# Gather of the up factors: tiles go round all eight PSUM banks, four copies of a T move from VectorE to ScalarE, and one sum goes ahead of the first copies

## The chip, the cores and the metric

The kernel runs on 1 core of one Trainium2 chip. The metric is the device time of one execution in microseconds. Engines are named as in the profile: PE is TensorE's matmul, PEld its weight load, DVE is VectorE, ACT is ScalarE, POOL is GpSimd, SP the engine that issues the DMAs. A name with a q behind it (PEldq) is the sequencer of that engine: it computes registers, waits for semaphores, branches, and hands the matmuls on.

## What is computed

A block of a perceiver on 32 sequences of 64 rows of 512 numbers: cross attention to 1601 context rows, causal self attention, and a mixture of experts whose weights are Kronecker factors. In the reference's words, cut to what matters here:

```python
x = x + xattn(layernorm(x), ctx_1024, ...)
x = x + attn(layernorm(x), ...)
x = x + ffn(layernorm(x), ...)

def kmoe(x_flat, W_router, A, B, scale, bias, ...):      # 2048 rows of 1024 numbers
    logits = x_flat @ W_router.T                          # 64 experts
    vals, idx = jax.lax.top_k(logits, top_k)              # top_k = 2
    probs = jax.nn.softmax(vals, axis=-1)
    xs = x_flat.reshape(-1, d_in1, d_in2)
    Ag = A[idx]
    Bg = B[idx]
    Y = jnp.einsum('nkoi,nij,nkpj->nkop', Ag, xs, Bg)
    out = jnp.einsum('nkop,nk->nop', Y, probs).reshape(-1, d_out1 * d_out2)
    return out * scale + bias
```

ffn is kmoe up (32x32 to 64x64), an exact gelu, and kmoe down (64x64 to 32x32). The change is in how Ag and Bg of the up layer are fetched.

## The kernel before

All engines run programs of their own that meet at semaphores; nothing is scheduled by a planner, the order on each engine is the order of the code. Cross attention comes first, then self attention over eight quads of rows, then the mixture. The last quad's output projection leaves its two halves in PSUM banks 2 and 3; VectorE adds them to the rows (`with_attended`, line 838, counted by the semaphore `se_r2`). A sum with the output bias (line 842), the layer norm and the stores of that last quad are done by VectorE inside the first part of the mixture.

The up layer runs for T = 0 to 3, 256 tokens with two experts each. Every T begins with a gather. A one-hot of the tokens' choices is multiplied by the experts' tables, so that PSUM holds the chosen factors: v = 0 is the factor A, v = 1 the factor B, q = 0 to 7 is an eighth of the table. So a T has 16 tiles, in the order (q, v). A tile is 32 matmuls (line 2222) into two banks, one for each half hf. Then hf 0 is copied to SBUF by ScalarE (line 2104) and hf 1 by VectorE (line 1947). The tile (q, v) uses banks 4v and 4v + 1, in each q again. Thus four banks are in use, and a tile waits until the copies of the tile two before it are done: `gather_up` waits for `s_geu` of both engines (`mo_geu0`, `mo_geu1`) at the tile's count less two. It also waits for `s_ts`: GpSimd has laid the tile's part of the table (line 1836) into one of two buffers.

PE's gather is a loop in hardware: one turn is two q, that is four tiles, and four turns are a T. All its counts are computed in registers. `apart` puts a step of its own before the tile's first matmul that carries the last waits (line 50 in the profile).

Behind the loop PE waits for the down layer's one-hots of the T before (`mo_ohedn0`, `mo_ohedn1`: they were transposed into banks 6 and 7) and, but for the last T, for `se_r2`. It then transposes the next T's rows (`rows`, line 1490) into ROW_BANKS, banks 2, 3, 6 and 7, which the gather doesn't use. It waits for the last copies of the gather. For T > 0 it computes the down router's logits of the T before in banks 0 and 1 (`logits_dn(0)`, line 2200; VectorE's `parts` reads them), and then the next T's up router (line 1506) and the 16 steps of the two contractions (lines 2239 and 2257), which use all banks.

VectorE's program in a T: for T > 0 one half of the rows is transposed (2.2 us) before the first copy, and a quarter of the other half (0.7 us) after the copies of q = 1, 2, 3 and 4. For T = 0, `with_attended` for bank 3 stands behind the two copies of q = 0, and the two sums of line 842 behind q = 2 and q = 4.

Of the kernel before, what the change touches and what calls it, by code (L numbers as in the profile page):

```python
# [27 lines left out]
P = 128  # L28
# [87 lines left out]
class Signals:  # L116


    CREDIT = 8
# [1147 lines left out]
def mixture_parts(sem, arena, over, area, low, top_area, early, ps, ident, h_at, tables):  # L1267
# [53 lines left out]
    ROW_BANKS = (2, 3, 6, 7)  # L1321
# [32 lines left out]
    def gathered_up(v, q, hf):  # L1354

        dst = fac[v].rearrange("p (m o) -> p m o", o=F1)[:, :, 32 * hf + 4 * q:32 * hf + 4 * q + 4]
        return dst, ps[:, 4 * v + hf, :].rearrange("p (o m) -> p m o", o=4)
# [224 lines left out]
    f.ROW_BANKS = ROW_BANKS  # L1582
# [70 lines left out]
def mixture(nc, block, arena, early, ps, a, first, rest, out):  # L1653
# [41 lines left out]
    ROW_BANKS = first.ROW_BANKS  # L1695
# [241 lines left out]
    def _(vec):  # L1937
# [4 lines left out]
        def gather_out(T, q, v):  # L1942
            if T and q == 0:
                vec.wait_ge((s_sta, s_stb)[v], STEPS * T + AHEAD)
            vec.wait_ge(s_gu, 16 * T + 2 * q + v + 1)
            dst, src = gathered_up(v, q, 1)
            vec.tensor_copy(dst, src).then_inc(s_geu[1], 1)
# [56 lines left out]
        for T in range(T_N):  # L2004
            if T:
                transposed(vec, T, 0)
            for q in range(8):
                for v in range(2):
                    gather_out(T, q, v)
                if T and 1 <= q <= 4:  # L2010
                    transposed(vec, T, 1, q - 1, 4)
                if T == 0:
                    if q == 0:
                        rest.with_attended(vec, 1)
                    if q == 2:
                        rest.with_output_bias(vec, 0)
                    if q == 4:
                        rest.with_output_bias(vec, 1)
# [4 lines left out]
            if T:  # L2023
                parts(T, 0)
# [73 lines left out]
    def _(act):  # L2098
        def gather_out(T, q, v):
            if T and q == 0:  # L2100
                act.wait_ge((s_sta, s_stb)[v], STEPS * T + AHEAD)
            act.wait_ge(s_gu, 16 * T + 2 * q + v + 1)
            dst, src = gathered_up(v, q, 0)
# [90 lines left out]
    def _(pe):  # L2194
# [16 lines left out]
        def gather_up(v, g):  # L2211

            pe.wait_ge(s_ts, g * 2 + v + 1)
            for e in range(2):
                pe.wait_ge(s_geu[e], g * 2 + v - 1 + CREDIT)
            apart(pe, SPARE)
            for o in range(4):
                for c in range(C):
                    for hf in range(2):
                        r = slice(hf * E, (hf + 1) * E)  # L2220
                        x = ohx_up[r, 0, :, c * R:(c + 1) * R] if v == 0 else ohx_b[r, c % 2, c // 2]
                        last = pe.matmul(ps[c * R:(c + 1) * R, 4 * v + hf, o * P:(o + 1) * P],  # L2222
# [131 lines left out]
        with pe.Fori(0, T_N) as T:  # L2354
# [4 lines left out]
            with pe.Fori(T * 4, T * 4 + 4) as j:  # L2359
                for r in range(2):  # L2360
                    gather_up(0, j * 2 + r)
                    gather_up(1, j * 2 + r)
            for e in range(2):
                pe.wait_ge(s_ohe["dn"][e], T - 1 + CREDIT)
            with pe.If(T < T_N - 1):
                pe.wait_ge(rest.r2, rest.r2_all)
                for t in range(2):
                    rows(pe, T + 1, t, ROW_BANKS[2 * t:2 * t + 2])
            for e in range(2):
                pe.wait_ge(s_geu[e], T * 16 + 16 + CREDIT)  # L2370
            with pe.If(T > 0):
# [3 lines left out]
                logits_dn(0)  # L2375
# [70 lines left out]
```

## Time and profile before

| | us |
|---|---|
| median of 3 runs | 1257.72 |
| lowest and highest | 1257.55, 1258.91 |
| the profiled execution's own time | 1257.94 |
| its span | 1255.9 |
| gather of T = 0, 1, 2, 3, first matmul from the span's start | 837.43, 895.95, 954.25, 1013.50 |

The profile is one execution. PE is busy for 1194.3 us of the span, DVE 799.6, ACT 435.9, POOL 274.4. Cross attention takes the first two fifths, self attention ends near 837 us, the up layer near 1067 us, and the down layer the rest. A timeline merges instructions of one line that follow each other closely; xN counts records, and one matmul of the gather leaves two records on PE, so 64 records are a tile. In brackets stands the idle time of the engine before the row, and what ended it. The sequencer's steps are not counted as busy; the view of a line shows them with their own duration (minimum, median, maximum), but not the time between one and the next.

### The profile page before, as it was taken

To read this page: it belongs to the slowest core of one execution; us is meant where nothing else is said; L and a number is where in the kernel's file an instruction comes from. 1 tells how busy PE (TensorE), PEld (TensorE's weight loads), DVE (VectorE), ACT (ScalarE), POOL (GpSimd) and SP (SyncE) were. 2 spreads that over 40 slices of the span, in tenths; PEclk is the share of its full clock that TensorE was granted. 3 is DMA by queue.
4 is the path that set the end of the run, shared out by engine and by line. 5 is a ranking of instruction groups with operands and counts; after the bars stand their busy time and mean duration, and the time that the engine had idled before them with its cause. 6 is when DMAs were issued, how large, how long until landed. Compare 5 with 4: busy or idle time off the path is not lost.

```text
span 1255.9 us, 63911 instructions
## 1 busy us (share of the span) xinstructions
PE 1194.3 (95%) x28911; PEld 797.9 (64%) x28911; DVE 799.6 (64%) x1612; ACT 435.9 (35%) x894; POOL 274.4 (22%) x477
## 2 busy tenths in 40 slices
PE   9999999999999999999999999997898988899995
PEld 6865443444444334666676667766787877789995
DVE  5566787678767773355555555575848576467775
ACT  2322311131113212312221222235656556466664
POOL 1000000000000001112221222114443525245655
PEclk9999999999999999999999999999999999999998
DMA  7887999999999992510111011410413122143423
GB/s 286 277 273 229 313 321 308 303 305 329 301 322 299 321 334 94 120 68 0 67 67 67 7 59 50 126 41 14 166 60 134 67 95 106 38 132 113 122 58 77
DMA packets 64977, 203.09 MB, mean 162 GB/s; under 512 B 12112, under 2 KB 28496, under 8 KB 51440
## 3 DMA queue, kind: packets, MB, share of 16 engines
q1 hardware_dynamic: 64880, 201.77, 49.2%
q8 instruction: 64, 1.05, 0.3%
q14 instruction: 33, 0.27, 0.1%
HBM read 168.18 MB, written 33.55 MB: 161 GB/s over the span
## 4 chain that ended last, share of the span: by engine, by line
PE 84%; DVE 5%; issue 3%; SPq 2%; POOL 2%; DMA 2%; ACT 1%; POOLq 0%; DVEq 0%; ACTq 0%
PE ps L738 14%; PE ps L581 12%; PE ps L1111 9%; PE ps L2222 5%; PE ps L2305 5%; PE ps L2271 5%; PE ps L251 5%; PE ps L1225 4%; PE ps L1132 4%; PE ps L494 3%; PE ps L2200 2%; PE ps L2318 2%; PE ps L2257 2%; DVE arena L1956 2%; DVE arena L593 2%
## 5 line engine op out<-in xcount | busy, mean ns | idle before, releaser
L593 DVE STREAM_TRANSPOSE arena<-arena 128x448 f32<-128x448 f32 (+1 forms) x512 | 258.7, 574 | 54.9 <-DMA arena<-ctx 36.1
L581 PE MATMUL ps<-arena 32*64 32x400 f32 (+1 forms) x4096 | 188.7, 501 | 2.7 <-DVE arena L593 1.9
L738 PE MATMUL ps<-arena 128*64 128x512 f32 x832 | 189.1, 598 | 0.0
L581 PEld LDWEIGHTS ps<-arena 32*64 32x64 f32 x4096 | 81.8, 131 | 102.6 <-DVE arena L593 50.8
L616 ACT ACTIVATE arena<-ps,arena 128x384 f32<-128x384 f32 x64 | 36.3, 581 | 291.3 <-DVE arena L607 291.3
L738 PEld LDWEIGHTS ps<-arena 128*64 128x64 f32 x832 | 55.6, 136 | 121.3 <-issue 121.3
L1111 PE MATMUL ps<-arena 128*128 128x256 f32 x512 | 114.2, 381 | 0.8 <-ACT arena L1046 0.8
L1111 PEld LDWEIGHTS ps<-arena 128*128 128x128 f32 x512 | 96.4, 190 | 17.2 <-issue 3.3
L911 POOL TENSOR_TENSOR arena<-arena 128x1024 f32<-128x1024 f32 x8 | 18.9, 2367 | 390.5 <-PE ps L738 390.5
L2120 ACT COPY arena<-ps 128x512 f32<-128x512 f32 x128 | 75.0, 586 | 50.3 <-PE ps L2271 26.5
L1956 DVE SCALAR_TENSOR_TENSOR arena<-ps,arena 128x512 f32<-128x512 f32 x64 | 69.8, 1120 | 33.7 <-PE ps L2257 33.2
L2222 PE MATMUL ps<-arena 64*32 64x128 f32 x4096 | 68.7, 273 | 7.9 <-issue 4.4
L2271 PE MATMUL ps<-arena 64*64 64x32 f32 x4096 | 71.0, 219 | 3.2 <-issue 3.2
L2271 PEld LDWEIGHTS ps<-arena 64*64 64x64 f32 x4096 | 69.7, 136 | 3.8 <-issue 3.4
L2222 PEld LDWEIGHTS ps<-arena 64*32 64x32 f32 x4096 | 58.1, 105 | 18.9 <-issue 14.7
L1966 DVE COPY arena<-ps 128x512 f32<-128x512 f32 x64 | 44.3, 692 | 37.9 <-PE ps L2305 35.7
L599 DVE TENSOR_REDUCE arena<-ps 128x1 f32<-128x401 f32 (+1 forms) x64 | 32.3, 567 | 54.7 <-PE ps L581 54.7
L979 DVE SCALAR_TENSOR_TENSOR arena<-ps,arena 128x512 f32<-128x512 f32 x32 | 20.6, 686 | 70.1 <-PE ps L1122 70.1
L929 POOL TENSOR_TENSOR arena<-arena 128x512 f32<-128x512 f32 x32 | 33.3, 1042 | 138.6 <-DVE arena L996 138.6
L2305 PE MATMUL ps<-arena 64*64 64x128 f32 x1792 | 62.7, 277 | 0.0
L251 PE MATMUL ps<-arena 128*128 128x512 f32 x128 | 60.2, 605 | 0.0
L1132 PE MATMUL ps<-arena 128*64 128x256 f32 x512 | 59.0, 380 | 0.0
(161 smaller groups left out, 1882.6 us busy)
## 6 DMA issues: line engine op xcount, KB each, us to landing
arena<-ctx SPq DMA_DIRECT2D x64, 1024.0 KB
arena<-ctx SPq DMA_DIRECT2D x32, 768.0 KB
arena<-q_n SPq DMA_DIRECT2D x64, 256.0 KB, 11.3
h_n<-arena SPq DMA_DIRECT2D x12, 1024.0 KB, 4.4
arena<-h_n SPq DMA_DIRECT2D x12, 1024.0 KB, 5.1
arena<-x SPq DMA_DIRECT2D x16, 512.0 KB, 4.4
arena<-ctx SPq DMA_DIRECT2D x32, 256.0 KB
x_n<-arena SPq DMA_DIRECT2D x16, 512.0 KB, 3.5
```

Source lines behind the costliest of these rows:

```text
L251: x = pe.matmul(ps[:, par, :], early.ats[:, c, par::2], early.xwv[:, c, :], start=c == 0, stop=c == DC - 1)
L581: last = pe.matmul(ps[b * SEQ:(b + 1) * SEQ, tb, 0:WIDTH[tb]], qs[p % 2][r, db, b * SEQ:(b + 1) * SEQ], z[PLACE[at]][r, b, 0:WIDTH[tb]], s ...
L593: vec.transpose(z[PLACE[at]][:, :, g * 224:g * 224 + nt * 32].rearrange("p b (j t) -> p b j t", t=32), slots[slot_of(k)][:, :, 0:nt, db * ...
L738: last = pe.matmul(ps[b * SEQ:(b + 1) * SEQ, OB, :], probt[:, j, b * SEQ:(b + 1) * SEQ], slot[:, b, jj, :], start=j == 0, stop=j == TILES - 1)
L1111: last = pe.matmul(ps[:, bank, m % 2 * QROWS:(m % 2 + 1) * QROWS], w[n][:, c, m * P:(m + 1) * P], lnt[:, c, :], start=c == 0, stop=c == DC ...
L1132: last = pe.matmul(ps[e * SEQ:(e + 1) * SEQ, 2 + pair, s2 * 256:(s2 + 1) * 256], lnt[:, c, at:at + SEQ], w["swv"][:, c, :].rearrange("p (m ...
L1225: last = pe.matmul(ps[:, (OUT if more else LAST_OUT) + par, :], aot[:, c, par::2], w["swo"][:, c, :], start=c == 0, stop=c == DC - 1)
L1956: vec.scalar_tensor_tensor(h[:, q, :, at].rearrange("p j g -> p g j"), ps[:, b:b + 2, :].rearrange("p b (g x) -> p (b g) x", x=2 * F1)[:, ...
L2120: act.copy(mid[u].rearrange("p (b x) -> p b x", b=2), ps[:, 2 * u:2 * u + 2, 0:256]).then_inc(s_me, 1)
L2222: last = pe.matmul(ps[c * R:(c + 1) * R, 4 * v + hf, o * P:(o + 1) * P], tab_st[v][r, o, :], x, start=True, stop=True)
L2271: last = pe.matmul(ps[k * F1:(k + 1) * F1, 2 * u + t, g * D1:(g + 1) * D1], st_h[u][rows_t, g * F1:(g + 1) * F1], two(st_a[u])[rows_t, k, ...
L2305: last = pe.matmul(ps[q * E:(q + 1) * E, 6 + hf, o * P:(o + 1) * P], slots_dn[slot][r, o, :], oh_st[r, 2 * q:2 * q + 2, :].rearrange("p k ...
```

## The change

- `ROW_BANKS` becomes (0, 1, 4, 5), and a tile (q, v) uses banks 4v + 2(q mod 2) and the one behind it: four tiles in flight, and a tile waits for the copies of the tile four before it.
- `PAST_DVE = (1, 2, 3, 4)`: for these q the hf 1 copy of v = 1 is made by ScalarE, ahead of its own hf 0 copy. VectorE's count goes up by 2 at its v = 0 copy, so that the counts stay.
- For T = 0, `with_attended` for bank 3 stands ahead of VectorE's first copy.
- On PE the waits for `se_r2` and for the down one-hots stand inside the loop, between its first and second q, since the second q now uses banks 2, 3, 6 and 7. Before each half of `rows` stands a wait for the copies of q = 6.
- `logits_dn` of the loop and `parts` use banks 2 and 3.

```diff
-    ROW_BANKS = (2, 3, 6, 7)
+    ROW_BANKS = (0, 1, 4, 5)
+    PAST_DVE = (1, 2, 3, 4)
@@ gathered_up
-        return dst, ps[:, 4 * v + hf, :].rearrange("p (o m) -> p m o", o=4)
+        return dst, ps[:, 4 * v + 2 * (q % 2) + hf, :].rearrange("p (o m) -> p m o", o=4)
@@ VectorE
             dst, src = gathered_up(v, q, 1)
-            vec.tensor_copy(dst, src).then_inc(s_geu[1], 1)
+            vec.tensor_copy(dst, src).then_inc(s_geu[1], 2 if q in PAST_DVE else 1)
@@
+            if T == 0:
+                rest.with_attended(vec, 1)
             for q in range(8):
-                for v in range(2):
+                for v in range(1 if q in PAST_DVE else 2):
                     gather_out(T, q, v)
                 if T and 1 <= q <= 4:
                     transposed(vec, T, 1, q - 1, 4)
                 if T == 0:
-                    if q == 0:
-                        rest.with_attended(vec, 1)
@@
-                parts(T, 0)
+                parts(T, 2)
@@ ScalarE
             act.wait_ge(s_gu, 16 * T + 2 * q + v + 1)
+            if v and q in PAST_DVE:
+                dst, src = gathered_up(v, q, 1)
+                act.copy(dst, src)
             dst, src = gathered_up(v, q, 0)
             act.copy(dst, src).then_inc(s_geu[0], 1)
@@ PE
-        def gather_up(v, g):
+        def gather_up(v, g, r2):
             pe.wait_ge(s_ts, g * 2 + v + 1)
             for e in range(2):
-                pe.wait_ge(s_geu[e], g * 2 + v - 1 + CREDIT)
+                pe.wait_ge(s_geu[e], g * 2 + v - 3 + CREDIT)
@@
-                        last = pe.matmul(ps[c * R:(c + 1) * R, 4 * v + hf, o * P:(o + 1) * P],
+                        last = pe.matmul(ps[c * R:(c + 1) * R, 4 * v + 2 * r2 + hf, o * P:(o + 1) * P],
@@
             with pe.Fori(T * 4, T * 4 + 4) as j:
-                for r in range(2):
-                    gather_up(0, j * 2 + r)
-                    gather_up(1, j * 2 + r)
-            for e in range(2):
-                pe.wait_ge(s_ohe["dn"][e], T - 1 + CREDIT)
+                gather_up(0, j * 2, 0)
+                gather_up(1, j * 2, 0)
+                pe.wait_ge(rest.r2, rest.r2_all)
+                for e in range(2):
+                    pe.wait_ge(s_ohe["dn"][e], T - 1 + CREDIT)
+                gather_up(0, j * 2 + 1, 1)
+                gather_up(1, j * 2 + 1, 1)
             with pe.If(T < T_N - 1):
-                pe.wait_ge(rest.r2, rest.r2_all)
                 for t in range(2):
+                    for e in range(2):
+                        pe.wait_ge(s_geu[e], T * 16 + 13 + t + CREDIT)
                     rows(pe, T + 1, t, ROW_BANKS[2 * t:2 * t + 2])
@@
-                logits_dn(0)
+                logits_dn(2)
```

PE's program inside the gather's loop, from the second tile of a turn to the third, in the kernel before. An ISA row here is a fused computation of registers. Where a row waits for two semaphores, a step that only waits stands before it and is not listed.

```order
L2213 REGISTER_ALU
L2215 REGISTER_ALU [waits mo_ts]
L2222 MATMUL ps<-arena 32x128 [waits mo_geu0,mo_geu1]
L2222 MATMUL ps<-arena 32x128 x31
L2213 ISA
L2215 REGISTER_ALU [waits mo_ts]
L2222 MATMUL ps<-arena 32x128 [waits mo_geu0,mo_geu1]
L2222 MATMUL ps<-arena 32x128 x31
```

The same place in the changed kernel.

```order
L2217 REGISTER_ALU
L2219 REGISTER_ALU [waits mo_ts]
L2226 MATMUL ps<-arena 32x128 [waits mo_geu0,mo_geu1]
L2226 MATMUL ps<-arena 32x128 x31
L2368 REGISTER_ALU [waits se_r2]
L2217 ISA [waits mo_ohedn1,mo_ohedn0]
L2219 REGISTER_ALU [waits mo_ts]
L2226 MATMUL ps<-arena 32x128 [waits mo_geu0,mo_geu1]
L2226 MATMUL ps<-arena 32x128 x31
```

Two steps of the sequencer have come between these two tiles: the REGISTER_ALU of line 2368 and the unlisted one that waits for `mo_ohedn1`. The other waits ride on steps that were there. From the loop's end to the first matmul of `rows` there are as many steps as before.

VectorE's program at the start of the gather of T = 0, in the kernel before (838 is `with_attended`, 842 the output bias, 1947 a copy out of a tile).

```order
L838 TENSOR_TENSOR arena<-ps,arena 128x512 [waits se_o]
L1936 UNCONDITIONAL_BRANCH
L1947 COPY arena<-ps 128x128x4 [waits mo_gu] x2
L838 TENSOR_TENSOR arena<-ps,arena 128x512 [waits se_o]
L1947 COPY arena<-ps 128x128x4 [waits mo_gu] x4
L842 TENSOR_TENSOR arena<-arena 128x512 [waits se_r2]
L1947 COPY arena<-ps 128x128x4 [waits mo_gu] x4
```

The same place in the changed kernel (the copy is line 1948 there).

```order
L838 TENSOR_TENSOR arena<-ps,arena 128x512 [waits se_o]
L1937 UNCONDITIONAL_BRANCH
L838 TENSOR_TENSOR arena<-ps,arena 128x512 [waits se_o]
L1948 COPY arena<-ps 128x128x4 [waits mo_gu] x4
L842 TENSOR_TENSOR arena<-arena 128x512 [waits se_r2]
L1948 COPY arena<-ps 128x128x4 [waits mo_gu] x2
L842 TENSOR_TENSOR arena<-arena 128x512 [waits se_r2]
```

The second sum now stands ahead of the copies, and fewer copies stand between the sums.

## Rows read from the trace of the kernel before

**Rows 1.** The page: busy time, and the chain that ended last.

```profile
PE 1194.3 (95%) x28911; PEld 797.9 (64%) x28911; DVE 799.6 (64%) x1612; ACT 435.9 (35%) x894; POOL 274.4 (22%) x477
...
PE 84%; DVE 5%; issue 3%; SPq 2%; POOL 2%; DMA 2%; ACT 1%; POOLq 0%; DVEq 0%; ACTq 0%
```

**Rows 2.** Busy time by stretch, one stretch for each T's gather.

```profile
core 0: us, PE busy (x) PEld busy (x) DVE busy (x) ACT busy (x) POOL busy (x), PEclk, DMA share, GB/s
...
895.90:913.90 18.00, 17.08 (x1024) 14.52 (x1024) 13.71 (x20) 9.16 (x15) 4.32 (x15) 1.00 0.46 175
...
1013.50:1032.20 18.70, 17.15 (x1024) 14.50 (x1024) 14.46 (x21) 9.62 (x16) 4.28 (x15) 1.00 0.14 57
```

**Rows 3.** Timeline of PE, T = 1, T = 2 and T = 3.

```profile
start us, us, engine line op out<-in xcount [idle before <-releaser]
...
895.95 4.27 PE L2222 MATMUL ps<-arena 64*32 64x128 f32 x256 [1.82 <-DVE arena L1475]
900.50 4.27 PE L2222 MATMUL ps<-arena 64*32 64x128 f32 x256 [0.28 <-issue]
...
954.25 2.18 PE L2222 MATMUL ps<-arena 64*32 64x128 f32 x128 [0.23 <-issue]
957.11 2.21 PE L2222 MATMUL ps<-arena 64*32 64x128 f32 x128 [0.67 <-DVE arena L1947]
959.61 4.28 PE L2222 MATMUL ps<-arena 64*32 64x128 f32 x256 [0.29 <-issue]
...
1013.50 2.21 PE L2222 MATMUL ps<-arena 64*32 64x128 f32 x128 [0.27 <-issue]
1016.31 2.18 PE L2222 MATMUL ps<-arena 64*32 64x128 f32 x128 [0.59 <-DVE arena L1947]
```

**Rows 4.** Timeline of DVE at the start of T = 2.

```profile
954.24 2.22 DVE L1466 STREAM_TRANSPOSE arena<-arena 128x1024 f32<-128x1024 f32 x1
956.36 1.24 DVE L1947 COPY arena<-ps 128x512 f32<-128x512 f32 x2
```

**Rows 5.** Timeline of ACT in T = 1, tiles 5 to 8.

```profile
902.73 0.58 ACT L2104 COPY arena<-ps 128x512 f32<-128x512 f32 x1 [0.40 <-PE ps L2222]
903.79 0.64 ACT L2104 COPY arena<-ps 128x512 f32<-128x512 f32 x1 [0.47 <-PE ps L2222]
904.82 0.58 ACT L2104 COPY arena<-ps 128x512 f32<-128x512 f32 x1 [0.39 <-PE ps L2222]
906.25 0.64 ACT L2104 COPY arena<-ps 128x512 f32<-128x512 f32 x1 [0.84 <-PE ps L2222]
```

**Rows 6.** Line 2213: PE's sequencer (PEldq) between two tiles.

```profile
L2213 PEldq ALU_OP  x32: 32/32/32, 838.2 to 1030.8; - x32
L2213 PEldq FUSED_REGOPS  x16: 51/51/51, 839.2 to 1029.7; - x16
```

**Rows 7.** Line 2359, one turn of the loop, 899 to 900.5 us.

```profile
L2359 PEldq FUSED_REGOPS  x2: 37/50/64, 899.8 to 900.2; - x2
L2359 PEldq COMPARE_BRANCH  x1: 213/213/213, 899.9 to 899.9; - x1
```

**Rows 8.** Line 2364: the two steps that compute and wait.

```profile
L2364 PEldq ALU_OP  x4: 36/36/36, 856.1 to 1032.1; - x4
L2364 PEldq EVENT_SEMAPHORE  x4: 51/51/51, 856.2 to 1032.2; - x4
```

**Rows 9.** Chain in order of time, T = 1: start, us, what.

```profile
894.42 0.68 DVE arena L1475
895.10 0.85 issue
```

**Rows 10.** Timeline of PE, T = 0: first tiles, then the logits.

```profile
837.43 2.76 PE L2222 MATMUL ps<-arena 64*32 64x128 f32 x160
840.93 1.58 PE L2222 MATMUL ps<-arena 64*32 64x128 f32 x96 [0.74 <-issue]
...
864.02 2.83 PE L1506 MATMUL ps<-arena 128*64 128x128 f32 x24 [2.43 <-issue]
```

More of the change, by code:

```diff
@@ L1581, in mixture_parts @@
     f.ohx_b = ohx_b
-    f.ROW_BANKS = ROW_BANKS
+    f.ROW_BANKS, f.PAST_DVE = ROW_BANKS, PAST_DVE
     f.s_wr = s_wr
@@ L1694, in mixture @@
     ohx_b = first.ohx_b
-    ROW_BANKS = first.ROW_BANKS
+    ROW_BANKS, PAST_DVE = first.ROW_BANKS, first.PAST_DVE
     s_wr = first.s_wr
```

## The prediction

> **What bounds the kernel now.** I read the page first. PE is busy for 95% of the span and carries 84% of the chain that ended last; VectorE carries 5% of it and ScalarE 1% [rows 1]. Work taken from VectorE is worth something only where PE waits for VectorE, and anything that lengthens PE's own program counts in full. Next I read the busy time by stretch: in the gather of T = 1, 18.0 us long, VectorE is busy 13.7 and ScalarE 9.2, and T = 3 is much the same [rows 2]. Neither engine is full. The granted clock is 1.00, the higher of its two levels (2.4 GHz), and nothing here opens a long gap in which it could fall.
>
> Then the timeline of PE, for the waits that end late. In T = 1 a turn of four tiles is busy 4.27 us, the next begins 4.55 us after it, and no turn waits for another engine; the 1.82 us ahead of the first tile is a wait for the one-hots, which the change leaves alone [rows 3]. In T = 2 the third tile waits 0.67 us for VectorE, in T = 3 0.59 us [rows 3]. The timeline of VectorE says why: its 2.22 us transpose runs until 956.46, so the copy of tile 0 begins at 956.36, when tile 1 is nearly done, and with two tiles in flight tile 2 starts only at 957.11 [rows 3, 4]. These two waits are what the wider use of PSUM can remove.
>
> What sets the pace between? ScalarE starts its copy when a tile is complete, so its starts are PE's clock: tile to tile takes 1.03 us from v = 0 to v = 1, 1.06 into the next q, and 1.43 over the loop's turn [rows 5]. The 0.40 between 1.43 and 1.03 can be taken apart. At the short boundary the sequencer runs three steps: 32 and 32 ns of register arithmetic, both of the first kind in [rows 6], and one that waits, 51 ns [rows 8]: 115 ns. At the turn it runs five: two fused ones of 37 and 64 ns, a branch of 213 [rows 7], 36 and 51 as in [rows 8]: 401 ns. That is 286 more and two steps more; if each step also takes 60 ns that no row shows, 286 + 120 = 406 ns, which is the 0.40. The 60 ns has a second witness: between the end of the one-hot copy and the first tile of T = 1 lie 0.85 us [rows 9], in which the sequencer runs seven steps (51, 37, 51, 72, 70, 36, 51 ns by their lines, 368 in all, the kinds of [rows 6 to 8]), and 0.85 - 0.37 over eight spaces is 0.06. So the pace of the gather is set by PE's sequencer: each step put between two tiles is paid in full, because no stock of matmuls bridges it.
>
> **The change part by part.**
>
> *Four tiles in flight.* The two waits go. The second pair of tiles starts 957.11 - 954.25 = 2.86 us after the first in T = 2, and 1016.31 - 1013.50 = 2.81 in T = 3 [rows 3]; at the normal pace it would be 1.03 + 1.06 = 2.09. Gain 0.77 + 0.72 = 1.49 us. What is late next? Tile 4 would have to wait for the copy of tile 0, which ends near 957.0, and begins at 959.61 even now [rows 3, 4]. GpSimd's table takes effect only within its two buffers, as before. So nothing takes the place of these waits.
>
> *Steps inside the loop.* This is the largest term. Between the second and the third tile of each turn the sequencer gets two steps more: one register computation (36 ns) and one that only waits (51 ns) [rows 8], with 60 ns behind each: 0.207 us. There are 4 turns in each of 4 T: 16 x 0.207 = 3.31 us. What they wait for is long there: the down one-hots are of the T before, and `se_r2` is done before the third tile of T = 0 (below). Behind the waiting steps stand only matmuls of the same PE, so the price is theirs alone. In the first turn of T = 0 PE stands idle 0.74 us, two and a half tiles in, for nothing another engine does [rows 10]; I take that as a supply of instructions that is late, and a sequencer that is 0.2 us slower there runs into it 0.2 us less. That takes off between 0 and 0.21; I take 0.1. Bounds for one boundary: below, 0, if the steps hide behind queued matmuls; above, 0.40, what the two further steps of the turn cost now [rows 5]. I take 0.207, since it reproduces both the 0.40 and the 0.85.
>
> *Behind the loop.* The same waits leave this place and others come, step for step, ahead of the first half of `rows`. Before its second half two steps are new, but the first 8 transposes cover them. The copies of q = 6 they ask for are made before the last two tiles end. 0 us, and at most 3 x 0.2 if the cover were gone. T = 3 has no `rows`: two steps fewer, ahead of a wait for the last copies that hides them. 0.
>
> *Four copies to ScalarE.* It makes a hf 1 and a hf 0 copy after one tile, 0.6 us each, while the tile pair takes 2.09 us [rows 5]: 9.2 + 4 x 0.6 = 11.6 us busy of 18. VectorE falls by 4 x 0.69. The last three q are not touched, so what follows the gather finds its copies at the same distance behind PE. 0 us. VectorE's transposes of the next rows come up to a tile earlier, and so does the load behind them; PE waits for neither now. 0 us.
>
> *The sum ahead of the first copies.* It waits for PE's last projection, which is over when the gather begins at 837.43 [rows 10], and takes about as long as a copy of the same size, 0.6 to 0.7 us [rows 4]. The first tile is done no sooner than 1.03 us after that start, so the first copy is hardly held up, and banks 2 and 3 are free before tile 2, two tiles on. 0 us.
>
> **The sum.** +3.31 - 0.1 - 1.49 = +1.7 us. Against the profiled execution's own 1257.94 that is 1259.6; against the median 1257.72, which is 0.2 lower, 1259.4. I forecast 1259.4. Its own range, with 0.18 to 0.23 per boundary and the doubt at T = 0, is 1258.8 to 1260.1.
>
> **The rivals.**
>
> *The steps are hidden.* If PE had a stock of matmuls queued at each boundary, two steps of 0.1 us would cost nothing and the 1.49 us stay as a gain: 1257.72 - 1.49 = 1256.2. For it speaks that PE shows no idle time at the tile boundaries inside a turn; against it that the turn's longer steps appear in the pace to the last hundredth [rows 5, 7]. The Trainium skill (TensorE: Matmul & The Clock Gate, the table at its head) gives PE an engine queue 64 deep; a stock of that depth would hold more than the two steps, and by that rule the time would be this rival's. The trace disagrees here: 0.40 us of 0.40 is exposed [rows 5].
>
> *The waits stay.* If VectorE were late for a reason that four tiles don't cure, the 3.2 us would come without the gain: 1260.9. Nothing in VectorE's rows speaks for it; the copy of tile 0 is simply too late for tile 2.
>
> *The supply of instructions gets worse.* This is the slower side. PE's program has stalls that only its own supply explains, 0.74 us in the first turn and 2.43 us in the logits of T = 0 [rows 10]. The loop is two steps longer and all behind it has shifted. One stall more, or one lengthened, costs 0.74 to 2.4 us: 1260.2 to 1261.8. It decides from 0.8 us on, where the time passes 1260.24. For it: such stalls exist, where code is run for the first time. Against it: the shift is a few instructions among hundreds, and a stall can as well shrink.
>
> **How the numbers follow.** I give the forecast 0.67, the hidden steps 0.08, the waits that stay 0.07, the supply 0.18. What a measurement of this kernel can tell from no change is 0.2%, 2.5 us: below 1255.2 faster, above 1260.2 slower. The forecast's case lies inside but for a tail of 0.04 above; the hidden steps lie inside but for 0.04 below; the waits that stay and the supply lie above but for 0.03. Faster 0.04, same 0.70, slower 0.26. The range, 1256.9 to 1261.6, leaves out the hidden steps and the far end of the supply.
>
> **What would show it.** In the profile after: no wait for the VectorE copy ahead of the third tile in T = 2 and T = 3; starts of ScalarE's copies with 1.27 us in place of 1.06 into the second q of a turn, 1.03 and 1.43 unchanged; turns 4.76 us apart in place of 4.55; the gather of T = 1 longer by 0.8 us, that of T = 2 and T = 3 by 0.1 each; VectorE's busy time down by 11 us and ScalarE's up by 10. I am wrong if turns stay 4.55 us apart, if a new wait stands at tile 4, or if the stalls of T = 0 change by more than 0.3 us.

## The result

The changed kernel takes 1260.55 us (median of 20 executions, 1258.00 to 1262.55); the kernel before, beside it, 1256.05 (20, 1253.71 to 1261.77). The ratio is 1.0028, 95% interval 1.0018 to 1.0038: slower by 3.5 us, between 2.3 and 4.8 (the two medians differ by 4.5, the two means by 3.7). The forecast was 1259.4 us and a loss of 1.7 us. The time lies in the range, but the loss of 0.28% lies above the 0.2% that the forecast took for what can be told from no change; the interval begins at 0.18%. For "slower" I had given 0.26, for "within 0.2%" 0.70. So the likelier side did not come, and what the forecast left out is the main question of what follows.

The profiled execution of the changed kernel took 1258.12 us, span 1256.3. That is only 0.4 us more than the span before, 1255.9, so the loss of 3.5 us cannot be read from the two spans: the changed kernel's profile is 0.94 us ahead when the first gather begins (836.49 for 837.43), before anything that was changed, and its mean granted clock is 0.996 where it was 0.993. The comparison has to go stage by stage. The page's line that answers to the first of [rows 1]:

```profile
PE 1194.4 (95%) x28911; PEld 796.5 (63%) x28911; DVE 789.2 (63%) x1596; ACT 444.0 (35%) x910; POOL 275.1 (22%) x477
```

VectorE has lost 10.4 us, ScalarE has gained 8.1, PE has the same work. None of it moves the end. The timeline of PE, T = 1, to be held against [rows 3]:

```profile
895.77 4.51 PE L2226 MATMUL ps<-arena 64*32 64x128 f32 x256 [1.83 <-DVE arena L1476]
900.56 4.49 PE L2226 MATMUL ps<-arena 64*32 64x128 f32 x256 [0.28 <-issue]
...
914.88 1.31 PE L1491 MATMUL ps<-arena 128*128 128x128 f32 x10 [0.29 <-issue]
```

The first turn now takes 4.79 us, not 4.55 (the next two take 4.76 each), and the transposes of `rows` (line 1491) begin 19.11 us after the first matmul of the gather. In the kernel before it was 914.10 - 895.95 = 18.15. So T = 1 has lost 0.96 us. T = 2 and T = 3:

```profile
955.05 4.46 PE L2226 MATMUL ps<-arena 64*32 64x128 f32 x256 [0.27 <-issue]
959.83 4.46 PE L2226 MATMUL ps<-arena 64*32 64x128 f32 x256 [0.31 <-issue]
```

```profile
1014.23 4.49 PE L2226 MATMUL ps<-arena 64*32 64x128 f32 x256 [0.27 <-issue]
1019.01 4.52 PE L2226 MATMUL ps<-arena 64*32 64x128 f32 x256 [0.28 <-issue]
```

The gaps of 0.67 and 0.59 us ahead of the third tile are gone: 256 records stand in one row. The first turn takes 4.78 us where it took 959.61 - 954.25 = 5.36. Over the whole gather T = 2 has won 0.04 us and T = 3 has lost 0.13. T = 0, against [rows 10]:

```profile
836.49 2.96 PE L2226 MATMUL ps<-arena 64*32 64x128 f32 x159
839.86 1.60 PE L2226 MATMUL ps<-arena 64*32 64x128 f32 x97 [0.42 <-issue]
```

The stall in the first turn is 0.42 us where it was 0.74, and the gather has lost 0.51 us (856.15 - 836.49 = 19.66 to its transposes, before 856.58 - 837.43 = 19.15). All four: 0.51 + 0.96 - 0.04 + 0.13 = 1.56 us lost. The starts of ScalarE's copies, T = 1, against [rows 5] (line 2108 is the hf 0 copy, line 2106 the new one):

```profile
901.76 0.63 ACT L2108 COPY arena<-ps 128x512 f32<-128x512 f32 x1 [0.35 <-PE ps L2226]
902.79 0.59 ACT L2106 COPY arena<-ps 128x512 f32<-128x512 f32 x1 [0.40 <-PE ps L2226]
...
904.07 0.64 ACT L2108 COPY arena<-ps 128x512 f32<-128x512 f32 x1 [0.21 <-PE ps L2226]
905.10 0.59 ACT L2106 COPY arena<-ps 128x512 f32<-128x512 f32 x1 [0.40 <-PE ps L2226]
...
906.52 0.64 ACT L2108 COPY arena<-ps 128x512 f32<-128x512 f32 x1 [0.35 <-PE ps L2226]
```

Copy to copy of PE's tiles: 1.03, 1.28 (901.76 and 902.79 are the fifth and sixth tile of this T, 904.07 the seventh), 1.03, 1.42. The forecast had 1.03, 1.27, 1.03, 1.43. The two steps that were put there:

```profile
L2368 PEldq ALU_OP  x16: 32/32/32, 838.3 to 1030.3; - x16
L2368 PEldq EVENT_SEMAPHORE  x16: 51/51/51, 838.4 to 1030.4; - x16
```

So the gathers did nearly what was forecast, 1.56 us against 1.72. They are less than half of 3.5. The rest had to be found elsewhere. Between the gathers the two timelines agree within 0.1 us, but for T = 0, where the changed kernel takes 0.26 us more. The down layer's first loop, two turns of 128 matmuls (line 2289, 2293 after the change), does not. The kernel before:

```profile
1067.82 7.40 PE L2289 MATMUL ps<-arena 64*64 64x128 f32 x256 [1.05 <-issue]
...
1076.92 7.27 PE L2200 MATMUL ps<-arena 64*64 64x128 f32 x256 [0.68 <-ACT arena L1477]
...
1086.64 0.88 PE L2271 MATMUL ps<-arena 64*64 64x32 f32 x48
```

The changed kernel:

```profile
1068.60 3.90 PE L2293 MATMUL ps<-arena 64*64 64x128 f32 x128 [1.04 <-issue]
1073.69 3.99 PE L2293 MATMUL ps<-arena 64*64 64x128 f32 x128 [1.19 <-DVE arena L1967]
...
1079.38 7.70 PE L2204 MATMUL ps<-arena 64*64 64x128 f32 x256 [0.68 <-ACT arena L1478]
...
1089.50 0.87 PE L2275 MATMUL ps<-arena 64*64 64x32 f32 x46
```

Where one row of 7.40 us stood there are now two with a gap of 1.19 us between the turns, together 9.08. The timeline puts the gap down to VectorE, but the sequencer shows another: its register for the next turn was computed at 1071.5, and the branch back began only 1.6 us later, with no wait in between.

```profile
L2396 PEldq ALU_OP  x2: 32/32/32, 1071.5 to 1076.7; - x2
L2396 PEldq COMPARE_BRANCH  x2: 76/144/213, 1073.1 to 1076.8; - x2
```

The down router's logits behind it (line 2204) take 7.70 us, not 7.27. From the first loop's first matmul to the first one of line 2275 it is 1089.50 - 1068.60 = 20.90 us; in the kernel before 1086.64 - 1067.82 = 18.82. That is 2.1 us more, at a granted clock of 1.00 in both, and nothing of the change is there: only the place of this code in PE's program is another.

These 2.1 us are not all lost, though. This stretch ends just before two stalls that the shift has shortened. The kernel before, right behind it:

```profile
1089.13 0.43 PE L2271 MATMUL ps<-arena 64*64 64x32 f32 x16 [1.61 <-issue]
...
1093.36 0.53 PE L2271 MATMUL ps<-arena 64*64 64x32 f32 x18 [1.62 <-issue]
...
1095.34 1.10 PE L2271 MATMUL ps<-arena 64*64 64x32 f32 x64
```

The changed kernel:

```profile
1091.43 0.48 PE L2275 MATMUL ps<-arena 64*64 64x32 f32 x18 [1.07 <-issue]
...
1095.12 0.54 PE L2275 MATMUL ps<-arena 64*64 64x32 f32 x20 [1.07 <-issue]
...
1097.11 1.11 PE L2275 MATMUL ps<-arena 64*64 64x32 f32 x64
```

A group of this line is 64 records. From the first loop's first matmul to the third group it is 1097.11 - 1068.60 = 28.51 us, and 1095.34 - 1067.82 = 27.52 in the kernel before, again at a clock of 1.00 in both. So the shift costs 2.1 us up to the first group and gives 1.1 of them back by the third: 1.0 us net. Together the profiles account for 1.56 + 0.26 + 0.99 = 2.8 us, which lies in the measured interval of 2.3 to 4.8 but is not all of 3.5.

### The profile page after: what moved, and what is told of

Read it like the earlier page. It is cut to its first block, busy times and chain, and to the rows that moved or that the text cites. A ratio compares the mean times of both kernels' runs of the same rounds, so it can differ in the third digit from the quotient of the medians.

```text
span 1256.3 us, 63963 instructions
## 1 busy us (share of the span) xinstructions
PE 1194.4 (95%) x28911; PEld 796.5 (63%) x28911; DVE 789.2 (63%) x1596; ACT 444.0 (35%) x910; POOL 275.1 (22%) x477
## 4 chain that ended last, share of the span: by engine, by line
PE 83%; DVE 6%; issue 3%; DMA 3%; POOL 2%; SPq 1%; ACT 1%; POOLq 0%; DVEq 0%; ACTq 0%
PE ps L738 14%; PE ps L581 11%; PE ps L1111 9%; PE ps L2226 6%; PE ps L2309 5%; PE ps L251 5%; PE ps L2275 5%; PE ps L1225 4%; PE ps L1132 4%; PE ps L494 3%; PE ps L2204 2%; PE ps L2322 2%; DVE arena L593 2%; DVE arena L1957 2%; PE ps L2261 2%
## 5 line engine op out<-in xcount | busy, mean ns | idle before, releaser
L911 POOL TENSOR_TENSOR arena<-arena 128x1024 f32<-128x1024 f32 x8 | 18.9, 2368 | 389.7 <-PE ps L738 389.7
L979 DVE SCALAR_TENSOR_TENSOR arena<-ps,arena 128x512 f32<-128x512 f32 x32 | 20.6, 686 | 70.0 <-PE ps L1122 70.0
```

## The experiments

Two theories stood against each other. A: the steps in the loop cost what was forecast, and the rest is a late supply of instructions in the down layer, brought about by the shifted program. B: the rest is something of the change itself (a wait, the banks, the work moved to ScalarE), or the steps cost more than the gathers show.

**The change again.**

> The changed kernel once more, beside the kernel before on the same chip. In the two profiles the four gathers together grew by 1.6 us (0.5, 1.0, 0.0 and 0.1 for T = 0 to 3), while the timed runs differ by a ratio of 1.0028 (1.0018 to 1.0038), 2.3 to 4.8 us. Theory A: the change costs what the gathers show, +1.6 to +1.8 us, ratio 1.0013, and the timed difference was partly the spread of single runs. Theory B: something outside the gathers adds about 2 us, which two single profiles can't show because cross attention alone moves by about 1 us from one execution to the next: ratio 1.0028 again.

Measured: ratio 1.0025 (1.0010 to 1.0040). That is nearer to B's number, though the interval does not exclude A's. Gathers of T = 1 to 3 last 18.49, 18.54 and 18.57 us from first to last matmul, as in the first profile (18.55, 18.48, 18.55; before 17.63, 18.50, 18.43). The gap in the down layer's first loop is there again, 0.65 us:

```profile
1071.66 3.86 PE L2293 MATMUL ps<-arena 64*64 64x128 f32 x128 [1.00 <-issue]
1076.17 3.99 PE L2293 MATMUL ps<-arena 64*64 64x128 f32 x128 [0.65 <-ACT arena L2142]
```

**The steps alone.** The kernel before with the waits of PE inside its loop and banks, depth and copies as they were. As in the change, `with_attended` for bank 3 also goes ahead of the first copies for T = 0 (not in this cut):

```diff
             with pe.Fori(T * 4, T * 4 + 4) as j:
-                for r in range(2):
-                    gather_up(0, j * 2 + r)
-                    gather_up(1, j * 2 + r)
+                gather_up(0, j * 2)
+                gather_up(1, j * 2)
+                pe.wait_ge(rest.r2, rest.r2_all)
+                for e in range(2):
+                    pe.wait_ge(s_ohe["dn"][e], T - 1 + CREDIT)
+                gather_up(0, j * 2 + 1)
+                gather_up(1, j * 2 + 1)
-            for e in range(2):
-                pe.wait_ge(s_ohe["dn"][e], T - 1 + CREDIT)
             with pe.If(T < T_N - 1):
-                pe.wait_ge(rest.r2, rest.r2_all)
```

> The kernel before, with nothing but PE's waits moved into the loop, between its first and second q (and the sum ahead of the first copies, so that the wait for it isn't long). Banks, depth and copies are as before, so the two waits of T = 2 and 3 stay. Theory A (every sequencer step between two tiles is paid in full): turns 4.76 us apart in place of 4.55, every gather about 0.85 us longer, in all +3.3 to +3.7 us, ratio 1.0027 to 1.0030. Rival (the steps hide and the growth of the gathers comes from writing eight banks): 0.

Measured: ratio 1.0029 (1.0015 to 1.0044), the ratio that A had. The gathers of T = 0 to 3 are longer by 0.50, 0.85, 0.56 and 0.69 us, 2.6 in all and not the 3.3 to 3.7 that A had; the 3.6 us of the ratio are again more than the gathers show, here without a shift of the code behind the loop, and where the difference lies is not shown. T = 2 and 3 pay less because their VectorE wait stays, and the steps of that turn lie inside it:

```profile
955.50 2.21 PE L2222 MATMUL ps<-arena 64*32 64x128 f32 x128 [0.27 <-issue]
958.32 2.18 PE L2222 MATMUL ps<-arena 64*32 64x128 f32 x128 [0.61 <-DVE arena L1947]
```

The third tile starts 2.82 us after the first, as before (2.86). So in the first turn of T = 2 and T = 3 steps and waits hide one another; the forecast's sum takes them apart as 0.77 less and 0.21 more, which comes to the same when both are changed.

**The wider use of PSUM without the steps.** The changed kernel, with GpSimd waiting in PE's place; PE cannot start the third tile without GpSimd's table.

```diff
+                if q == 1:
+                    pool.wait_ge(rest.r2, rest.r2_all)
+                    for e in range(2):
+                        pool.wait_ge(s_ohe["dn"][e], T - 1 + CREDIT)
@@ PE
-                pe.wait_ge(rest.r2, rest.r2_all)
-                for e in range(2):
-                    pe.wait_ge(s_ohe["dn"][e], T - 1 + CREDIT)
```

> The changed kernel without the waits in PE's loop: GpSimd waits for the last quad's sums and for the down one-hots before it lays out the table of q = 1, and PE, which waits for that table anyway, gets no step more. Theory A: turns 4.55 us apart again, the waits of T = 2 and 3 gone, so -1.5 to -1.7 us against the kernel before, ratio 0.9988, and 3.3 us faster than the changed kernel. Rival (eight banks or the copies cost something themselves): no faster than the kernel before, ratio 1.000 or above.

> The kernel of pool_waits again: the changed kernel with GpSimd waiting in PE's place, no step more in PE's loop. The theory of the steps: gathers of T = 1 to 3 as before less the two VectorE waits, 1.5 us gained, ratio 0.9988. Rival (the wider use of PSUM gains nothing outside the two waits and loses some of it in the supply of instructions behind): ratio 0.9992 to 1.000, with the stretch from the down layer's first loop to its first contraction at 19.3 us or more.

Measured: 0.9994 (0.9981 to 1.0007), and the second time 0.9996 (0.9983 to 1.0009). The second profile, T = 2:

```profile
955.93 4.29 PE L2230 MATMUL ps<-arena 64*32 64x128 f32 x256 [0.27 <-issue]
960.51 4.25 PE L2230 MATMUL ps<-arena 64*32 64x128 f32 x256 [0.29 <-issue]
```

Turns are 4.58 us apart, without the wait: T = 1, 2, 3 last 17.72, 17.71 and 17.71 us from first to last matmul, where before it was 17.63, 18.50 and 18.43. The 1.5 us are there. From the down layer's first loop to line 2279 both profiles take 19.3 us, not 18.8, of which 0.42 stand in the logits (7.69 us for 7.27); but in the first of them, at a clock of 1.00, this is made up by the third group (27.48 us, before 27.52). A gain of 1.5 us lies within both intervals; neither excludes no change, so this version does not beat the kernel before by anything that was measured.

**Without ScalarE's extra copies.** The changed kernel with `PAST_DVE = ()`.

> The changed kernel, but all hf 1 copies stay on VectorE. Theory A: ScalarE's four extra copies are hidden and VectorE has time for its own, so the time is that of the changed kernel within 0.3 us, and no new wait stands at tile 4 in T = 2 and 3. Rival (VectorE falls behind when it also transposes): a wait for VectorE of some tenths of a us at tiles 4 to 8 of T = 1 to 3, up to +2 us.

Measured: 1.0030 (1.0019 to 1.0042), the same as the changed kernel within what these runs can tell. The third tile of T = 2 has no wait either, so the four tiles in flight are enough by themselves. The work moved between VectorE and ScalarE shows no worth here, either way.

**Four steps more.** Before the third tile of each turn of the changed kernel, behind the waits that the change put there:

```diff
+                for _ in range(5):
+                    apart(pe, SPARE)
                 gather_up(0, j * 2 + 1, 1)
```

Five are written; the first takes the place of the step that only waited, so four are added. The expectation speaks of the place between the third and the fourth tile; the kernel that ran has them between the second and the third, as this edit and the gap of 0.76 us in the rows below show. For the price of a step this makes no difference to what was expected.

> The changed kernel with four steps more of PE's sequencer in each turn of the gather's loop, between its third and fourth tile; each only counts a semaphore up, none waits. If a step costs its own 51 ns and 60 behind it and nothing hides them: 16 x 4 x 0.11 = 7.1 us more than the changed kernel, turns of the loop 5.20 us apart in place of 4.76, ratio to before 1.0085. If the steps overlap with matmuls still queued: less than 2 us more, ratio 1.004 at most, turns 4.76 to 4.9 us apart. If the price is the 36 to 51 ns of the steps alone: 2.3 to 3.3 us more, ratio 1.0048 to 1.0055, turns 4.90 to 4.96 us apart.

Measured: 1.0072 (1.0056 to 1.0087), 5.5 us over the changed kernel's 1.0028, and in the trace 10:

```profile
900.03 2.18 PE L2226 MATMUL ps<-arena 64*32 64x128 f32 x128 [1.81 <-DVE arena L1476]
902.98 2.18 PE L2226 MATMUL ps<-arena 64*32 64x128 f32 x128 [0.76 <-ACT arena L2108]
905.48 2.18 PE L2226 MATMUL ps<-arena 64*32 64x128 f32 x128 [0.33 <-issue]
```

```profile
L50 PEldq EVENT_SEMAPHORE  x5: 51/51/51, 907.3 to 907.9; - x5
```

A turn takes 5.45 us, not 4.79: 0.66 for four steps, 0.165 each. The five starts lie 0.6 us apart from first to last, so each comes 0.15 us after the one before though it is 51 ns long. The space behind such a step, which counts a semaphore up, is 0.10 us, not the 0.06 that I had taken for all. Nothing hides it, which settles the rival of the hidden steps. The gathers sum to 84.9 us from first to last matmul, against 74.7 in the changed kernel's first profile: 10.2 us. Part of the difference to the 5.5 us of the times stands in the down layer: its first loop, eight instructions later in the program, has gaps of 0.57 and 0.32 us, but of the two stalls behind it one is gone and one is 0.48 us, so that the third group comes 26.20 us after the loop's start, 2.3 us sooner than in the changed kernel. The rest is not explained; this kernel has only five executions in the comparison.

**The place in the program.** The kernel before once more, and the kernel before with four steps (five written) put once ahead of the loop over T:

> The kernel before, unchanged, as a second look at its own trace. In its first profile the down layer's first loop (256 matmuls) runs in 7.4 us without a gap, and its first contraction starts 18.8 us after that loop's first matmul; in the changed kernel and in steps_only that is 20.3 to 20.9. Theory A (the lost time outside the gathers is a supply of instructions that the longer PE program makes worse): again 7.4 us without a gap and 18.8 within 0.3. Rival B (that stretch varies from execution to execution whatever the kernel): somewhere between 18.8 and 20.9. Time ratio 1.000 within 0.0013 by both.

```diff
         pe.wait_ge(s_fold, 2)
+        for _ in range(5):
+            apart(pe, SPARE)
         with pe.Fori(0, T_N) as T:
```

> The kernel before, with four steps of PE's sequencer more, once, ahead of the loop over T: all that comes behind stands four instructions later in PE's program, as behind the loop of the changed kernel, and nothing is added inside any loop. Theory A (place in the program decides the late instructions of the down layer's first loop): that stretch takes 20.3 to 20.9 us in place of 18.8, the kernel is 1.5 us slower, ratio 1.0012. Rival B (it is the time, not the place): 18.8, ratio 1.0003 at most (0.4 us for the four steps). The gathers keep their lengths of 19.15, 18.15, 19.08 and 19.84 us within 0.2 by both, but for T = 0.

> The kernel of pad_once again (the kernel before with four steps once ahead of the loop over T), since in its first look the clock had fallen to half just where the late instructions of the down layer's first loop were to be seen. Theory A (place in the program): where the clock is 1.00 there, a gap of 0.65 to 1.2 us stands between the loop's two turns, as in all four profiles of the changed kernel and its variants that are four instructions longer; ratio 1.0006 to 1.0013. Rival B (it belongs to the changed timing): no gap, one row of 7.4 us, ratio 1.000 to 1.0003.

before_again: 1.0003 (0.9992 to 1.0015), one row of 7.37 us, 18.9 us in all. pad_once: 1.0013 (1.0000 to 1.0026), 21.0 us in all, but its profile cannot decide, since the granted clock had dropped just there (its loop has no gap between the turns):

```profile
core 0: us, PE busy (x), PEclk, DMA share, GB/s
...
1071.50:1073.50 2.00, 1.98 (x41) 0.55 0.03 8
1073.50:1075.50 2.00, 2.00 (x51) 0.59 0.00 0
```

pad_second: 1.0018 (1.0005 to 1.0031), clock 1.00, and the gap is there, as in the changed kernel:

```profile
1068.11 3.72 PE L2289 MATMUL ps<-arena 64*64 64x128 f32 x128 [1.05 <-issue]
1072.55 3.99 PE L2289 MATMUL ps<-arena 64*64 64x128 f32 x128 [0.71 <-ACT arena L2138]
```

Its logits take 7.70 us, as in the changed kernel.

The same steps between the up layer's loop and the down layer's first loop:

```diff
+        for _ in range(5):
+            apart(pe, SPARE)
         with pe.Fori(0, 2) as p:
             for b in range(4):
                 unit_first(p, b)
```

> The kernel before with the same steps between the up layer's loop and the down layer's first loop: everything up to there stands in its old place, the down layer's first loop four or five instructions later. Theory A (that loop's own place decides): the gap of 0.65 to 1.2 us between its two turns is there, gathers and their stalls as before, ratio 1.0008 to 1.0013 (0.4 to 0.7 us of it for the steps themselves, 0.15 each). Rival B: no gap, ratio 1.0003 to 1.0005.

Measured: 1.0017 (1.0005 to 1.0029):

```profile
1071.00 3.72 PE L2289 MATMUL ps<-arena 64*64 64x128 f32 x128 [1.81 <-issue]
1075.53 3.97 PE L2289 MATMUL ps<-arena 64*64 64x128 f32 x128 [0.80 <-DVE arena L1966]
```

The gap is there with everything up to the loop in its old place. Both ratios, 1.0018 and 1.0017, lie above what Theory A had (up to 1.0013), though the intervals reach down to it; their lower ends, 1.0005, also lie next to what Rival B had, so it is the profiles that decide here and not the times. In pad_behind it is the register step ahead of the branch that is late: it starts 3.9 us after the loop's first matmul, and the branch follows it at once. In the profiles at +4 with a gap that step starts at 2.9 us, and the branch is late. One instruction more in front, and the stall falls one instruction earlier in the loop: it keeps its place in the program while the code moves past it.

And the changed kernel with 245 instructions that a branch always skips:

```diff
         pe.wait_ge(s_fold, 2)
+        with pe.Fori(0, 2) as none:
+            with pe.If(none * none > none):
+                for _ in range(245):
+                    apart(pe, SPARE)
```

> The changed kernel with 245 instructions more ahead of the loop over T, which a branch always skips, with the two turns of a small loop about them: everything behind stands 252 instructions later than in the changed kernel, 256 later than in the kernel before. The records of the instruction queue show packets of 16384 bytes. Theory A (the place within such a packet decides the late instructions): the down layer's first loop runs as in the kernel before, 7.4 to 7.5 us in one row, and the time is 0.7 to 1 us below the changed kernel's but for some 0.8 us for the added branches: ratio to before 1.002 to 1.0025. Rival B (the changed kernel's timing, or the absolute place): the gap of 0.65 us or more stays, ratio 1.003 to 1.0035.

Measured: 1.0016 (1.0003 to 1.0028), below the expected 1.002 to 1.0025, which the interval holds. The gap is gone, the branch follows its register at once, and the logits take 7.27 us again:

```profile
1069.34 7.29 PE L2293 MATMUL ps<-arena 64*64 64x128 f32 x256 [1.04 <-issue]
```

```profile
L2400 PEldq ALU_OP  x2: 32/32/32, 1072.2 to 1075.8; - x2
L2400 PEldq COMPARE_BRANCH  x2: 76/150/223, 1072.3 to 1075.9; - x2
```

All profiles together, by how many instructions the down layer's first loop stands behind its old place, with the gap between its turns and the time from its first matmul to line 2271's first and third group (the third where the clock was 0.99 or more up to there):

| kernel | later by | gap, us | first group, us | third group, us |
|---|---|---|---|---|
| before, before_again | 0 | none, none | 18.8, 18.9 | 27.5, - |
| moved_256 | 256 | none | 18.8 | 26.7 |
| pool_waits, pool_again | 2 | none, none | 19.3, 19.3 | 27.5, - |
| after, after_again, no_shift | 4 | 1.19, 0.65, 0.66 | 20.9, 20.3, 20.1 | 28.5, 28.6, 28.2 |
| pad_second, pad_behind | 4, 5 | 0.71, 0.80 | 20.2, 19.9 | 28.4, 28.1 |
| more_steps | 8 | 0.57 and 0.32 | 20.6 | 26.2 |

Left out are pad_once and steps_only (0 later, 20.6 us), in whose profiles the clock was half for some 4 us at this place. The gap follows the place and neither the timing nor the change. It comes with 4 or 5 instructions wherever they are put, and goes when 252 are added to those 4. What it costs by the third group is 0.6 to 1.1 us, less than the 1.1 to 2.1 up to the first, since the stalls behind it move with the place too. The page's line of the instruction queue gives 1.05 MB in 64 packets, 16 KB each. The Trainium skill (TensorE: Matmul & The Clock Gate, Part 2) has a MATMUL instruction of 64 bytes. By that 256 instructions are one packet, which is an estimate; the trace agrees in so far as a shift by 256 brings the loop's old picture back. The two stalls behind the loop do not come back to 1.61 us, though (1.32 and 1.07 in moved_256), so the place within a packet is not all that counts. That the branch waits for a packet is argued from this; no row shows it waiting. For it speaks that in every kernel one packet of this queue starts between 1.3 and 2.2 us after the loop's first matmul, and that it took 1.45 us in the profile with the gap of 1.19, but 0.96 to 1.13 in the four with gaps of 0.65 to 0.80.

**Longer turns.** Since each boundary of the loop costs 0.40 us, the kernel of pool_waits with half as many:

```diff
-            with pe.Fori(T * 4, T * 4 + 4) as j:
-                gather_up(0, j * 2, 0)
-                gather_up(1, j * 2, 0)
-                gather_up(0, j * 2 + 1, 1)
-                gather_up(1, j * 2 + 1, 1)
+            with pe.Fori(T * 2, T * 2 + 2) as j:
+                for r in range(4):
+                    gather_up(0, j * 4 + r, r % 2)
+                    gather_up(1, j * 4 + r, r % 2)
```

> The kernel of pool_waits with the gather's loop in two turns of eight tiles in place of four turns of four; nothing else. Eight boundaries of 0.40 us (the branch and what it needs) go over the four gathers, and the code of the gather is twice as long. If a boundary is paid in full wherever it stands: gathers of T = 1 to 3 each 0.8 us shorter than in pool_waits (17.7 from first to last matmul to 16.9), 3.2 us in all less the code's first supply at T = 0, ratio to before 0.9965 if that supply costs nothing more. Rival: matmuls run for the first time are supplied too slowly, so that T = 0 gives back 1.4 to 2.8 us and the ratio is 0.998 to 0.9995.

Both expectations were far off: 1.0337 (1.0314 to 1.0360), 42 us slower. T = 1:

```profile
903.40 1.46 PE L2230 MATMUL ps<-arena 64*32 64x128 f32 x35 [4.07 <-issue]
908.09 3.66 PE L2230 MATMUL ps<-arena 64*32 64x128 f32 x125 [3.24 <-issue]
...
916.11 2.28 PE L2230 MATMUL ps<-arena 64*32 64x128 f32 x125 [1.59 <-issue]
...
922.39 8.43 PE L2230 MATMUL ps<-arena 64*32 64x128 f32 x512 [0.40 <-POOL arena L1837]
```

In the first of the two turns PE stands idle for 4.07, 3.24, 0.48, 1.59 and 1.73 us for instructions; the second turn (512 records) runs without a gap. In these stretches the granted clock falls as well: 0.93 over T = 1 and 0.94 over T = 2 and 3, where pool_again has 1.00, so part of the loss is matmuls at half clock behind the idle times (PE is busy for 56.4 us in T = 1 and not 53.4). The view of the DMA queues for one T (packets, MB, share), in T = 1, 899 to 954 us:

```profile
q8 instruction: 10, 0.16, 1.3%
```

In the kernel before the same stretch of T = 1, T = 2 or T = 3 has no row of this queue (another instruction queue, q14, has 1 to 3 packets there in both kernels), while T = 0 has six packets of it. I read this as the whole body of the loop over T being loaded in T = 0 and held. With 128 matmuls more it is no longer held, and each T loads about ten packets again.

## Why the prediction was right in its steps, and where it fell short

- *Steps inside the loop, 0.207 us each turn.* Right in place and in size. T = 1 gives 0.96 / 4 = 0.24, steps_only 0.85 / 4 = 0.21. By their starts in the trace (T = 1) the two new steps take 0.208 us until the next one begins, 32 + 65 and 51 + 60 ns, just as forecast; where a turn lost 0.24, the other 0.03 stands behind the fused step that was there before. The space of 0.10 us belongs to steps that count a semaphore up (more_steps), which the change doesn't add.
- *Four tiles in flight, 1.49 us.* Right: no wait at the third tile in T = 2 and 3, none at tile 4, turns as at T = 1. The traces of pool_waits and pool_again show it alone; their times do not tell it from nothing.
- *Stall at T = 0, -0.1.* Not shown either way. The gather has lost 0.51 us where 0.73 was forecast, but its stall differs between two profiles of the kernel before (0.74 and 1.03 us) and between two of the changed one (0.42 and 0.88). By the forecast's own sign of being wrong, a change of more than 0.3 us in the stalls of T = 0, it was wrong: 0.74 became 0.42, and the two in the logits went from 2.39 and 2.43 to 2.73 and 2.10. That sign was badly chosen, since the unchanged kernel's second profile has 2.82 and 2.20.
- *Four copies to ScalarE and the sum ahead: 0.* Right (no_shift).
- *Behind the loop: 0.* Right for the steps: between the gather and the contractions both timelines agree. **But this is the step that failed in what it did not price:** "all behind it has shifted" stood only in the third rival, with 0.18. Up to the first group the shift cost 2.1 us in the first profile and 1.3 to 1.5 in the next two, from a loop that had shown no stall before; net, by the third group, 1.0, 1.1 and 0.6. I had looked for stalls where they stood already, in T = 0, and called a shift by a few instructions among hundreds as likely a gain as a loss. Both came: one stall new, two shorter, and the sum a loss at +4 and a gain of 0.9 us at +256.
- *The rivals.* The hidden steps are refuted by more_steps, and with them any stock of queued matmuls as cover for steps between tiles. The waits did not stay. The supply got worse, at 0.6 to 1.1 us net against the 0.74 to 2.4 that I had priced, on top of the forecast and not in place of it: +1.6 in the gathers, +0.3 in the rest of T = 0 (both by the first pair of profiles) and +0.6 to +1.1 in the down layer are 2.5 to 3.0 us, against 3.5 measured (2.3 to 4.8). I had given the forecast and this rival as one or the other, each with a share; they should have been added. With 1.0 us for the shift the forecast would have been +2.7.
- *The sum's base.* The forecast was made on 1257.72; 20 executions of the same kernel gave 1256.05. Three executions of a kernel whose times run from 1253 to 1262 set the level no better than that. The absolute time was hit partly by luck: a base 1.7 us too high and a loss 2.8 us too small (4.5 by the medians) offset each other but for the 1.1 us by which the time was missed. The forecast's own range is also slightly off its terms, which give 1258.9 to 1259.9 and not 1258.8 to 1260.1.

Open is what the supply does between a packet's landing and the branch, why two or four instructions make the logits 0.4 us longer in most profiles, and where the last 0.7 us of the 3.5 stand.

## What to carry to other kernels

Where one engine's own program sets the pace, count each step its sequencer gets between two tiles inside a loop, at 0.10 to 0.15 us by its kind; put a wait on an engine that has time, as GpSimd had here. Ask of every edit what it does to the place and length of the code behind it, down to loops it does not touch, and carry such a comparison on until the two timelines run alike again: the 2.1 us up to one line were 1.0 us two groups later. Before a loop body is made longer, see in the instruction queue whether it is now held between turns.

## What the runs showed of the hardware that was not expected

- A step of PE's sequencer that only counts a semaphore up lasts 51 ns in its record and takes 0.15 to 0.165 us of the pace (more_steps); one that only waits for a semaphore long reached lasts 51 ns too and takes 0.11 (the changed kernel). The Trainium skill (Perfetto Trace Analysis, Sequencer-only Instruction) says that only the execution of such a step is in the profile, not what is before and behind it; the trace agrees, with 0.06 and 0.10 us behind.
- A loop over T whose body fits is loaded once; 128 matmuls more brought about ten packets of 16 KB and, by the starts of the gathers against pool_again, 11 to 13 us more for each T from T = 1 on, part of it at half clock.
- Code that runs for the first time can stall at a loop's branch back, 0.65 to 1.2 us, or not, by its place alone; the stalls behind it (1.61 and 1.62 us in the kernel before, 1.07 to 1.38 at +4 and +5, none above 0.5 at +8) change with the place as well.
- The clock differs between executions of one kernel. In before_again it was half for part of the stretches that follow idle times of PE (2.82 and 2.20 us in the logits of T = 0), with a mean of 0.63 over 10 us, and again near 1095 us (0.66 from 1092 to 1102); in the changed kernel's profile the first drop is smaller, the second is not there (1.00):

```profile
862.00:872.00 10.00, 6.69 (x193) 0.63 0.02 5
```

```profile
862.00:872.00 10.00, 7.65 (x347) 0.83 0.02 3
```

Over 103 executions of the kernel before (one of 5433 us left out), the mean granted clock lies between 0.988 and 0.996, and the time rises by 0.7 us for each 0.001 that it is lower. This makes up under half of the spread between executions (0.44 of the variance). The mean clock of the changed kernel's 20 executions is 0.992, against 0.993 for the kernel before, which is worth some 0.3 us of the loss by the same slope, an estimate.
